# One tile moved between two groups of experts' work in the last stage of a two-layer transformer block

## The reference, cut to what matters

```
x = x + tanh(g_xattn[0]) * L0_xattn(layernorm(x), ctx_1024)     # 16 heads
x = x + tanh(g_ffn[0])   * L0_ffn(layernorm(x))                 # each token: its 2 best of 8 experts
x = x + tanh(g_xattn[1]) * L1_xattn(layernorm(x), ctx_1024)     # 1 head, causal
x = x + tanh(g_ffn[1])   * L1_ffn(layernorm(x))

def L1_ffn(x):                                                  # Bz = 128, Sz = 64, E = 8
    capacity = max(1, int(Sz * 2.0 / E) + 1)                    # 17 tokens for each expert and sequence
    scores = softmax(einsum('bsd,ed->bse', x, router_w))
    gate_vals, sel_idx = top_k(swapaxes(scores, 1, 2), capacity)
    tokens = x[b_idx, sel_idx]
    h = gelu(einsum('becd,edh->bech', tokens, w1) + b1)         # 128 -> 512
    y = einsum('bech,ehd->becd', h, w2) + b2                    # 512 -> 128
    return zeros_like(x).at[b_idx, sel_idx].add(y * gate_vals[..., None])
```

## Time and profile before

| | |
|---|---|
| median of 3 runs | 1075.1 us (1072.61 to 1077.79) |
| profiled execution, its own time | 1075.1 us |
| its span in the profile | 1073.3 us |
| busy share: PE, PEld, DVE, ACT, POOL | 88%, 74%, 56%, 54%, 64% |

### The profile page before, as it was taken

How to read it: one execution, slowest core, us unless ns; L and a number is a source line. 1 busy time by engine, 2 the same in 40 slices (tenths; PEclk the granted TensorE clock), 3 DMA queues, 4 the chain that set the end, 5 groups by cost and what they waited for, 6 DMA issues and landing times.

```text
span 1073.3 us, 25309 instructions
## 1 busy us (share of the span) xinstructions
PE 949.7 (88%) x8941; PEld 795.5 (74%) x8941; DVE 604.6 (56%) x1554; ACT 583.7 (54%) x1258; POOL 689.0 (64%) x909
## 2 busy tenths in 40 slices
PE   4999998798768999899989998887899999999992
PEld 2677776676657998899979977775577666778881
DVE  4888889987953562144513557886544433533321
ACT  2878786677524445444544657654445455445440
POOL 5655566478737777177507777832476657878885
PEclk9999999999867999999999999989999999999996
DMA  9345232011144667677766775204164454475454
GB/s 353 98 138 172 98 130 103 14 51 43 50 151 148 208 213 246 202 207 208 221 198 199 237 227 177 79 33 126 10 112 48 71 85 47 68 114 54 50 55 44
DMA packets 132829, 136.58 MB, mean 127 GB/s; under 512 B 33634, under 2 KB 103650, under 8 KB 131810
## 3 DMA queue, kind: packets, MB, share of 16 engines
q1 hardware_dynamic: 102482, 97.52, 28.7%
q0 software_dynamic: 28928, 29.91, 17.1%
q10 hardware_dynamic: 1296, 7.54, 1.7%
HBM read 49.81 MB, written 49.62 MB: 93 GB/s over the span
## 4 chain that ended last, share of the span: by engine, by line
PE 53%; DVE 12%; ACT 9%; DMA 8%; POOL 7%; issue 6%; SPq 3%; POOLq 0%; ACTq 0%; DVEq 0%
PE psum L777 10%; PE psum L787 9%; PE psum L948 7%; PE psum L958 7%; ACT w_sb L1556 3%; PE psum L620 3%; DMA work<-w_sb 3%; PE psum L912 2%; DMA out_x<-ln_sb,dest 2%; DMA odd<-ln_sb,dest 2%; POOL xg L1834 2%; DVE mx L1069 2%; DVE w_sb L1075 1%; ACT lnT L1528 1%; ACT work L1563 1%
## 5 line engine op out<-in xcount | busy, mean ns | idle before, releaser
L1636 ACT ACTIVATE hid_sb<-psum,work 128x128 f32<-128x128 f32 (+1 forms) x424 | 145.8, 412 | 160.6 <-PE psum L777 156.7
L1849 POOL DMA_INDIRECT work<-yg,place x128 | 129.2, 1009 | 88.9 <-issue 81.6
L777 PE MATMUL psum<-work 128*128 128x128 f32 (+1 forms) x848 | 153.8, 325 | 11.0 <-DMA work<-w_sb 8.9
L787 PE MATMUL psum<-w_sb,hid_sb 128*128 x1192 | 151.1, 276 | 0.0
L787 PEld LDWEIGHTS psum<-w_sb,hid_sb 128*128 128x128 f32 x1192 | 145.4, 193 | 2.1
L777 PEld LDWEIGHTS psum<-work 128*128 128x128 f32 x848 | 125.1, 194 | 24.6 <-DMA work<-w_sb 14.5
L948 PE MATMUL psum<-work,w_sb 128*128 128x272 f32 (+2 forms) x512 | 132.2, 400 | 4.1 <-ACT ctx_sb L1750 2.1
L1925 POOL DMA_INDIRECT out_x<-ln_sb,dest x68 | 106.0, 1560 | 46.2 <-DVE ln_sb L1476 26.8
L1262 DVE TENSOR_TENSOR yg_sb<-psum,work 128x128 f32<-128x128 f32 (+1 forms) x106 | 36.7, 346 | 169.7 <-PE psum L787 167.2
L1750 ACT ACTIVATE ctx_sb<-psum,w_sb 128x272 f32<-128x272 f32 (+2 forms) x256 | 116.0, 488 | 26.1 <-PE psum L948 22.5
L1925 POOL DMA_INDIRECT odd<-ln_sb,dest x68 | 105.7, 1555 | 36.4 <-DVE ln_sb L1476 17.0
(11 more groups left out here) (214 smaller groups left out, 1771.1 us busy)
## 6 DMA issues: line engine op xcount, KB each, us to landing
work<-w_sb SPq DMA_DIRECT2D x106, 322.0 KB
work<-xg SPq DMA_DIRECT2D x73, 128.0 KB
yg<-yg_sb SPq DMA_DIRECT2D x73, 128.0 KB
xg<-yg_sb SPq DMA_DIRECT2D x24, 384.0 KB, 4.0
ctx_sb<-tok SPq DMA_DIRECT2D x8, 1088.0 KB, 6.1
ctxn<-sums_sb SPq DMA_DIRECT2D x64, 64.0 KB
out_x<-x_sb SPq DMA_DIRECT2D x16, 256.0 KB
odd<-yg_sb SPq DMA_DIRECT2D x10, 384.0 KB, 2.7
```

What stands on the lines that cost most here:

```text
L777: e.matmul(banks[UP_BANKS[c]][:, 0:cols], w1g(b)[:, c * P:c * P + P], xgT_sb[:, u % 2, at:at + cols], start=True, stop=True).then_inc(s_up, 1)
L787: ins = e.matmul(banks[DOWN_BANKS[b % 2]][:, n * D:n * D + D], hid0[:, b % 2, c, n * P:n * P + P], w2_sb[:, bass.ds(number, 1), c, :].rear ...
L1636: e.activation(hid0[:, b % 2, c, 0:cols], banks[UP_BANKS[c]][:, 0:cols], ACT.Gelu, bias=w1g(b)[:, HID + c:HID + c + 1]).then_inc(s_hg, 1)
L1849: e.indirect_dma_start(dst[:, k, :], None, yg_dram[h], at, bounds_check=NROWS[h] - 1, oob_is_err=False).then_inc(s_get[i], 16)
```

## The change

```diff
-SIZES = (8, 8, 9, 9, 8, 8, 7, 7)
+SIZES = (8, 8, 8, 9, 8, 8, 8, 7)
 FIRST = [sum(SIZES[:sg]) for sg in range(NSG + 1)]
```

## The result

| | before | after |
|---|---|---|
| median of 14 runs | 1075.71 us (1071.58 to 1080.74) | 1081.56 us (1078.34 to 1089.81) |
| profiled execution: time, span | 1075.1, 1073.3 us | 1083.73, 1081.9 us |
| ratio of the runs | | 1.0054, 95% interval 1.0036 to 1.0072 |

The changed kernel is slower by 5.8 us, 0.54%. The interval is 3.9 to 7.7 us. The forecast was 1080.5 us, 5.4 us above the median shown then.

A forecast was written before the change was run, and what follows sets the result against it. GpSimd's scatter queue was taken as the bound: 1075.1 us, +14.9 for 8 more scatters behind step 40, -1.5 idle time, -8.2 for step 40's earlier start, +0.2 for landings, gives 1080.5 us; range 1076 to 1085.

The forecast's parts named there:

- Terms (a) to (d): TensorE reaches step 42 6.6 us earlier: fewer tiles in group 2, fewer chunks in group 3, one gather less, routing 0.
- case 3: Rival: gap ahead of step 16 stays, VectorE's lists being late; 2.1 us less gained, 1082.6 us; inside the forecast's 0.70.
- The queue on GpSimd: GpSimd, 1.8 us behind at step 40 before, owes nothing there after the change: step 40 starts another 1.8 us earlier.
- The second way to the sum: Counted from step 24: 11 us more GpSimd idle time, less a start 5.8 us earlier, gives 5.2 us.
- term (b): Group 3's 8 steps turn two chunks instead of three, 0.11 us less each: 0.9 us earlier.
- (d): Fourth batch's routing starts one step later, but its TensorE work all ends ahead of step 40: 0.
- Costed at nothing: Group 2 and 6 columns, result buffers, group 5's destinations, the accumulate's landings at step 49; only 0.2 us taken, for landings.
- case 1: Rival: landings at step 49 cost their 1.7 us and destinations come 2 us late, 1084 us; chance 0.13.
- The four result buffers: Gating waits for scatters of four steps ago; about steps 48 to 51 those landed 1 to 4 us ahead of need.
- Case 2: Rival: each of 16 picks in groups 5 and 6 holds GpSimd 0.35 us, 5.6 us: 1086 us; chance 0.03.
- Case 4: Rival: scatter number unchanged, GpSimd idles no more, only step 24's earlier start (5.8 us) counts: 1069.3 us; chance 0.04.
- Case 5: Rival: waits around routing shrink too, step 40 starts up to 3 us earlier than reckoned, 1077.5 us; chance 0.10.

The follow-up runs named there:

- even: Changed kernel with 8 tiles in every group, which puts three chunks in the last group; last scatter at stage time 326.66 us, ratio 1.0082 to the kernel before.
- extra_g5: Kernel before plus one more accumulating scatter in each step of group 5, 8 in all; last scatter at 330.30 us, ratio 1.0143.
- drop_after: Changed kernel without the third chunk's 8 scatters in group 5; last scatter at 315.42 us, ratio 0.9995 to the kernel before.
- after_again: The changed kernel run again, nothing altered; last scatter at 322.58 us, ratio 1.0052 to the kernel before.
- g5short: Kernel before with one tile moved from group 5 to group 6, chunks in place; last scatter at 316.84 us, ratio 0.9993.
- drop_before: Kernel before without the third chunk's 8 scatters in group 3; last scatter at 317.27 us, ratio 1.0005.
- extra_g3: Changed kernel plus one more accumulating scatter in each step of group 3, 8 in all; last scatter at 324.69 us, ratio 1.0081 to the kernel before.
- g2long: Changed kernel with 9 tiles in group 2 and 8 in group 3, same chunks; last scatter at 323.39 us, ratio 1.0032 to the kernel before.

## Why the prediction was right, point by point

- **The bound.** GpSimd's queue of scatters, not TensorE. Shown from both sides: of the versions that only change sizes even has the earliest TensorE and ends last; extra_g5 and drop_after move the end by GpSimd's work alone.
- **The pitch, 1.858 us, and the accumulate's 0.93 us.** (965.01 to 1069.89 is 104.88 us; 55 x 1.858 + 3 x 0.93 is 104.98.) They held in every version.
- **The added 14.9 us and the idle time removed, 1.5 us.** 104.88 us against 91.59 us before is +13.3 us, 13.4 forecast. Measured.
- **Terms (a) to (d), 6.6 us.** Step 42's up matmul is at 213.92 us for 220.51: 6.6 us. The gap ahead of step 16 is again 1.10 us (834.89 to 835.99), so case 3, the gap that doesn't close, is out. The third transpose and the longer gating (0.56 us for 0.42) cost 0.25 us as taken.
- **The queue on GpSimd, 1.8 us.** Step 40's scatter starts 965.01 - 964.23 = 0.8 us behind its gating: caught up. The start is 8.15 us earlier for 8.2.
- **The second way to the sum** came to the same total with two errors that cancel: the first scatter of step 24 is 7.0 us earlier and not 5.8 (888.04 - 747.38 = 140.66 us against 891.87 - 744.25 = 147.62), and the added idle time is 12 us and not 11. Step 24's up matmul is 6.5 us earlier (125.50 us for 131.98) and step 32's 6.4 us (169.38 us for 175.75), so the 0.9 us of term (b) don't show between them: part of the fourth batch's routing now lies behind step 24, which (d) rightly sets to nothing at step 40, but which counts at step 24. The first sum doesn't pass through that step.
- **Costed at nothing.** The destinations (0.16 us, ahead of the gating at 963.66) were there in time. Landings behind the big accumulate, 1015 to 1030 us:

```profile
DMA to landing us min/median/max: 3.2/3.3/6.0
```

6.0 us at most, and no pause in GpSimd's timeline. The 0.2 us that I took for it are 0, and case 1 is refuted for this kernel. Its sign was set wrong, though: "it decides when landings pass 5.6 us", and one did. The 6.0 us are those of step 50's first scatter (1018.82 us); the one that waits for it, step 52's first, comes 4 pitches later, at 1026.29 us, 7.5 us behind. The 3 pitches hold for a step's last scatter only, and that one (1020.72 us) took 4.5 us. The landing waits it was built on do exist (947.01 and 952.07 us, 1.36 and 1.69 us), in group 4, where GpSimd idles anyway.
- **The four result buffers.** At steps 48 to 51 no gating waits for a landing, as reckoned. The last two do, steps 62 and 63 (1054.88 and 1058.34 us), 2.49 and 2.48 us; in the kernel before none does. Their first scatters start 9 us behind their gating, so it costs nothing.
- **Case 2, GpSimd locked out of descriptor writing by VectorE.** Scatters beside picks (out_x, then odd, 962 to 995 us; 16 of these 17 are of group 5):

```profile
L1925 POOL DMA_INDIRECT out_x<-ln_sb,dest x9 | 14.0, 1553 | 3.6 <-issue 2.1 <-DVE ln_sb L1476 1.2 <-DMA odd<-ln_sb,dest 0.3
L1925 POOL DMA_INDIRECT odd<-ln_sb,dest x8 | 12.3, 1544 | 2.4 <-issue 2.4
```

1553 and 1544 ns, as without picks; over all 24 of group 5 (965 to 1009 us) 1554 and 1547 ns. The picks themselves are not all alike: their first operation took 0.35 to 0.70 us there (0.70 at 979.41 us), which nothing on GpSimd waited for and whose cause was not tried. The Trainium skill (SBUF — State Buffer, section "SBUF: two separate sides") has GpSimd kept from writing descriptors while VectorE runs an operation in a two-port mode, and names a fp32 copy from SBUF to SBUF as one that goes into it. The prediction took this for every one-input fp32 operation; whether the picks run in that mode no run shows. As a cost on the scatters it is not borne out by the trace here.
- **Case 4, only the number of scatters counts.** All versions of the sizes have 136 scatters; their ends span 10 us. Refuted.
- **Case 5** would have step 40 earlier than 8.2 us; it is not.
- **The size.** Stage +5.1 us, tail +0.3 us, sum 5.5 us; 5.8 us between the medians and 5.4 us forecast. The tail has no term in the prediction: from the last scatter's start to the end, 12.0 us for 11.7. It is the same in after_again (12.0 us), and the last accumulate starts 3.9 us behind the last scatter in both kernels, so what is longer lies behind it. It was 11.1 to 13.1 us over the versions with two chunks in the last group, and what sets it was not tried. The 0.2 us taken for landings and the 0.3 us left out nearly cancel, which is luck. On "slower or no change", which the forecast split evenly, the ratio of 1.0054 falls just on the slower side, but its interval reaches from 1.0036 to 1.0072, so which side it is isn't settled by the runs.

No version beats the kernel before beyond what its measurement can tell. g5short is the earliest in the stage with all work done, by 0.5 us. Every version with two chunks in the last group ends 28.8 us behind step 56's first scatter, and with 57 tiles to be done ahead of it step 56 can't start much earlier: the changed kernel without its third chunks gets there 1.9 us before the kernel before, and ends 1.95 us before it.

## What to carry to other kernels

When two engines share a loop and their loads per step vary, the end is the largest, over all steps, of "when this step's input is ready" plus "what the slower queue still has to do from there"; a heavy step is free ahead of a slack stretch, and behind the last one it is paid, less the idle time that it fills. The same 14.9 us of scatters were worth 0.1 us (drop_before) and 2.2 us (extra_g3) ahead of the slack, and 7.1 us (drop_after) and 12.9 us (extra_g5) behind or in it. So put the heavy steps early, and read the place of the last pause in the queue that ends last. Groups as even as possible for one engine can be the worst choice for the other.

## What the runs showed that was not expected

The first four experiments ran on a chip on which the stages ahead of the last took far longer: the kernel before took 1294.18 us there (30 runs, 1285.04 to 1300.76), and in g2long's profile the last stage began at 957.93 us. Stretches of g2long, then of the kernel before on the usual chip (columns as in the earlier trace rows):

```profile
0.00:200.00 200.00, 171.44 (x3112) 131.62 (x3116) 163.17 (x246) 139.77 (x227) 113.48 (x253) 0.97 0.42 147
200.00:400.00 200.00, 149.08 (x1773) 121.16 (x1761) 116.40 (x228) 84.91 (x145) 116.62 (x164) 0.80 0.21 69
400.00:600.00 200.00, 121.38 (x777) 106.91 (x777) 40.76 (x140) 52.58 (x149) 93.55 (x95) 0.79 0.42 128
```

```profile
0.00:200.00 200.00, 171.83 (x3146) 131.41 (x3147) 165.33 (x253) 141.64 (x230) 113.87 (x253) 0.99 0.42 148
200.00:400.00 200.00, 167.31 (x2033) 146.43 (x2033) 140.66 (x320) 103.50 (x194) 143.25 (x191) 0.88 0.35 113
400.00:600.00 200.00, 190.41 (x1446) 180.05 (x1445) 70.93 (x221) 96.22 (x284) 111.19 (x134) 0.99 0.70 214
```

The first 200 us are alike. From 200 to 600 us TensorE, VectorE and ScalarE have less to do in the same time, the granted clock falls from 0.88 and 0.99 to 0.80 and 0.79, and the DMA engines move 69 and 128 GB/s for 113 and 214. The last stage isn't touched: even's last scatter had a stage time of 326.66 us on that chip and 326.65 us on another. What slows the middle stages on that chip was not looked into; the experiments' comparison is with the kernel before on the same chip.
